# Output weights of a two-layer post-norm kernel: one block sooner, and the last two blocks as the larger of a sign and a comparison

## What is computed

```python
x = L0_attn_x                                   # 8 x 512 tokens, width 512
x = layernorm(x + x @ (W + delta_W).T)
# ternary_quant: scale = mean(|W|); clip(round(W / (scale + 1e-8)), -1, 1) * scale
z = x @ ternary_quant(W_syn).T + b_syn          # 2048 wide
thresh = top_k(z, k=204)[-1]
hidden = where(z >= thresh, relu(z), 0)
out = hidden @ ternary_quant(W_out).T + b_out
x = layernorm(layernorm(x + out, gamma, beta))
```

## Time and profile before

| | us |
|---|---|
| median of 3 runs | 633.77 (632.89 to 633.91) |
| the profiled execution | 634.05 |
| its span, from the first to the last instruction | 632.3 |
| TensorE busy | 586.0 (93%) |
| ScalarE busy | 544.0 (86%) |
| VectorE busy | 539.4 (85%) |
| GpSimd busy | 376.3 (60%) |
| granted TensorE clock, mean | 0.976 |

### The profile page before, as it was taken

How to read it: one execution, slowest core, us unless ns; L and a number is a source line. 1 busy time by engine, 2 the same in 40 slices (tenths; PEclk the granted TensorE clock), 3 DMA queues, 4 the chain that set the end, 5 groups by cost and what they waited for, 6 DMA issues and landing times.

```text
span 632.3 us, 8712 instructions
## 1 busy us (share of the span) xinstructions
PE 586.0 (93%) x2482; PEld 266.3 (42%) x2482; DVE 539.4 (85%) x657; ACT 544.0 (86%) x724; POOL 376.3 (60%) x712
## 2 busy tenths in 40 slices
PE   8799669999999999999999999999999999997573
PEld 7434324444444444444444444444444444443221
DVE  5796998998998899888888888898998888899882
ACT  1797659999999999999999999999999999989942
POOL 0126386777776547585565457545857555757773
PEclk9999789999999999999999999999999999999887
DMA  8982234545465454555454554545564454434462
GB/s 331 320 263 51 50 83 85 116 91 129 100 109 126 66 118 87 113 101 133 95 124 100 103 117 73 123 78 125 102 133 90 95 101 100 79 74 83 91 95 80
DMA packets 184581, 71.66 MB, mean 113 GB/s; under 512 B 168144, under 2 KB 176336, under 8 KB 183888
## 3 DMA queue, kind: packets, MB, share of 16 engines
q1 hardware_dynamic: 184528, 71.07, 51.2%
HBM read 20.72 MB, written 8.39 MB: 46 GB/s over the span
## 4 chain that ended last, share of the span: by engine, by line
PE 71%; DVE 8%; issue 6%; POOL 6%; ACT 3%; DMA 1%; DVEq 0%; POOLq 0%; ACTq 0%
PE z_ps L972 27%; PE o_ps L992 15%; PE u_ps L955 14%; PE o_ps L985 14%; ACT junk L542 2%; DVE w_sb L772 1%; DVE w_sb L815 1%; DVE z_sb L801 1%; POOL tmp L423 1%; DVE m L777 1%; POOL nmean L374 1%; POOL b L388 1%; ACT hh L579 1%; DVE hT L751 1%; POOL rs L384 1%
## 5 line engine op out<-in xcount | busy, mean ns | idle before, releaser
L542 ACT ACTIVATE junk<-z_sb,t_col 128x2048 f16<-128x2048 f32 x128 | 255.1, 1995 | 10.8 <-POOL t_col L442 9.8
L972 PE MATMUL z_ps<-t_syn,xhT 128*128 128x512 f16 x1024 | 231.0, 379 | 2.7 <-DVE t_syn L663 2.7
L972 PEld LDWEIGHTS z_ps<-t_syn,xhT 128*128 128x128 f16 x1024 | 99.8, 98 | 134.3 <-issue 18.1
L985 PE MATMUL o_ps<-t_out,hT 128*128 128x512 f16 x512 | 122.4, 395 | 16.8 <-DMA hT<-hh 12.4
L955 PE MATMUL u_ps<-weff,xT_sb 128*128 128x512 f32 x256 | 117.5, 602 | 2.3 <-ACT x1s L561 2.3
L992 PE MATMUL o_ps<-t_out,hT 128*128 128x512 f16 x512 | 116.1, 380 | 0.0
L423 POOL TENSOR_SCALAR tmp<-signs,dev 128x1 f32<-128x1 f32 x64 | 40.3, 629 | 124.3 <-ACT junk L542 123.4
L801 DVE SCALAR_TENSOR_TENSOR z_sb<-z_ps,sc,bias_z 128x1024 f32<-128x1024 f32 x64 | 82.0, 1280 | 18.4 <-PE z_ps L972 18.2
L772 DVE SCALAR_TENSOR_TENSOR w_sb<-z_sb,t_col 128x2048 f32<-128x2048 f32 x32 | 86.6, 2707 | 6.4 <-POOL t_col L442 6.2
L542 ACT ACTIVATE junk<-z_sb,start 128x2048 f16<-128x2048 f32 x32 | 64.0, 2001 | 29.7 <-DVE z_sb L801 29.7
L985 PEld LDWEIGHTS o_ps<-t_out,hT 128*128 128x128 f16 x512 | 51.5, 101 | 83.1 <-issue 16.0
(11 more groups left out here) (118 smaller groups left out, 605.4 us busy)
## 6 DMA issues: line engine op xcount, KB each, us to landing
xT_sb<-in_xT SPq DMA_DIRECT2D x16, 512.0 KB, 4.0
out_y<-y_sb SPq DMA_DIRECT2D x32, 256.0 KB, 2.9
z_sb<-in_w_synT SPq DMA_DIRECT2D x4, 1024.0 KB, 12.3
hh<-in_w_outT SPq DMA_DIRECT2D x2, 1024.0 KB, 9.6
z_sb<-in_w_outT SPq DMA_DIRECT2D x2, 1024.0 KB, 10.5
hT<-hh SPq DMA_TRANSPOSE x66, 4.3
weff<-in_wT SPq DMA_DIRECT2D x2, 512.0 KB, 4.7
w_sb<-in_dwT SPq DMA_DIRECT2D x2, 512.0 KB, 5.6
```

The lines of the kernel that those rows point to most:

```text
L542: a_.activation(junk[:, n % 2, :], z_sb[:, t % ZS, :], ACT.Sign, bias=at, scale=-1.0, accum_out=signs[:, j, r:r + 1]).then_inc(counted, 1)
L972: last = mm(z_ps[:, c, b * BANK:(b + 1) * BANK], xhT[:, j, h * KD + k, :], t_syn[:, k, n0:n0 + BANK], start=k == 0 and h == 0, stop=k == K ...
L985: mm(o_ps[t % OS][:, :], hT[:, j, 0, c, :], t_out[:, c, :], start=c == 0, stop=False)
```

## The change

1. On TensorE, total() for the output weights moves ahead of mm2(1,1).
2. On VectorE, out_scale and out_weights(0) move ahead of evac(1,1), and out_weights(1) from behind top8(0) to behind evac(1,1).
3. Blocks 2 and 3 are made by sign: ScalarE makes sign(w - half the scale), VectorE the comparison times -1 and then the larger of both. Block 2 takes the place between top8(0) and select(0), block 3 stands ahead of lo_h(0) and no longer behind it.
4. On ScalarE the two signs are put into stage 1: behind count(1,1) and behind ln1_out. In stages 1 and 2 count(s,3) goes ahead of hi_h(s-1).
5. On TensorE, mm3_lo of tile 0 goes ahead of flags(1).

```diff
+EARLY3 = 2
+        side_out = [hT[:, k, 1 - k, :, :].rearrange("p k t -> p (k t)") for k in range(2)]
+            def sign_out(k):
+
+                act.wait_ge(out_scaled, 1)
+                wait(act, t_out_made, k - 1)
+                a_.activation(side_out[k % 2], out_in[k], ACT.Sign, bias=sc[:, 10:11]).then_inc(over_out, 1)
+
...
                 if live(s):
                     count(s, 1)
+                    if s == 1:
+                        sign_out(2)
                     second_step(s)
...
                 if live(a):
                     ln1_out(s, a)
+                if s == 1:
+                    sign_out(3)
+                if s <= EARLY3:
+                    count(s, 3)
                 if live(s - 1):
                     hi_h(s - 1)
-                if live(s):
+                if live(s) and s > EARLY3:
                     count(s, 3)
...
+            def out_weights_by_sign(k):
+
+                wait(dve, t_out_made, k)
+                link(v.tensor_scalar(neg_out, out_in[k], sc[:, 10:11], -1.0, ALU.is_lt, ALU.mult))
+                dve.wait_ge(over_out, k - 1)
+                v.tensor_tensor(t_out[:, QB * k:QB * (k + 1), :].rearrange("p c d -> p (c d)"), side_out[k % 2], neg_out,
+                                ALU.max).then_inc(t_out_made, 1)
...
             lo_x(2)
-            evac(1, 1)
             out_scale()
             out_weights(0)
+            evac(1, 1)
+            out_weights(1)
 
             below(0)
             top8(0)
-            out_weights(1)
+            out_weights_by_sign(2)
             select(0)
...
             evac(2, 1)
-            out_weights(2)
+            out_weights_by_sign(3)
             lo_h(0)
-            out_weights(3)
...
             mm1(3)
+            total(o_ps[2][:, 0:1], part_out[:, :], part_summed, 2)
             mm2(1, 1)
-            total(o_ps[2][:, 0:1], part_out[:, :], part_summed, 2)
             mm1(4)
...
                     mm3_hi(l)
+                if l == 0:
+                    mm3_lo(l)
                 if live(f):
                     flags(f)
-                if live(l):
+                if live(l) and l > 0:
                     mm3_lo(l)
```

More of the change, by code:

```diff
@@ L175, in postln_kernel @@
         scaled = sem("scaled")
+        out_scaled = sem("out_scaled")
+        over_out = sem("over_out")
         over = sem("over")
@@ L745, in out_scale @@
                 link(v.tensor_scalar(sc[:, 9:10], sc[:, 8:9], 1e-8, 0.5, ALU.add, ALU.mult))
-                link(v.tensor_scalar(sc[:, 10:11], sc[:, 9:10], -1.0, None, ALU.mult))
+                v.tensor_scalar(sc[:, 10:11], sc[:, 9:10], -1.0, None, ALU.mult).then_inc(out_scaled, 1)
+                dve.wait_ge(out_scaled, 1)
                 link(v.tensor_scalar(sc[:, 11:12], sc[:, 5:6], sc[:, 8:9], X_SCALE / H_LIMIT, ALU.mult, ALU.mult))
```

## The result

| | before, us | changed, us |
|---|---|---|
| median, ten runs of each side by side | 633.69 (632.89 to 634.10) | 636.21 (634.80 to 640.26) |
| the profiled execution (span) | 634.05 (632.3) | 636.56 (634.8) |
| busy: TensorE, ScalarE, VectorE, GpSimd | 586.0, 544.0, 539.4, 376.3 | 585.6, 547.7, 537.8, 365.0 |

The ratio is 1.0049, with a 95% interval from 1.0037 to 1.0060: **slower by 0.5%**, 2.5 us, where 1.4 us less was forecast. The time lies above the whole range.

The account below looks back on a forecast made before the run. The prediction took the fill's chain to `ok` of tile 3, through the small engines, as the bound: 0.7 + 0.65 = 1.35 us sooner, so 633.77 - 1.35 = 632.4 us (unseen sizes: 632.4 to 633.1); range 630.8 to 634.4.

Parts of the forecast that it names:

- its L423 is held until 53.0, its last instruction until 55.5: Tile 0's second correction on GpSimd, held by VectorE's moved pair; count(0,3) then starts at about 55.7, 2.9 us late.
- The maximum: VectorE's new maximum of two fp16 tensors in blocks 2 and 3, replacing a 2.35 us instruction: 1.23 us, at most 1.39.
- tile 1's third correction: On GpSimd, three blocking VectorE instructions instead of five: about 6 us instead of 10, count(1,4) 4.4 us sooner.
- count(2,3) held hi_h(1) back: ScalarE in stage 2: hi_h(1) waits behind count(2,3) and starts at 93.9 against 94.57, so 4.4 us become 0.7.
- TensorE stopped inside mm2(4): New TensorE stop from 96.1 to 99.5, as mm2(4,1) waits for evac(3,1).
- the 0.65: First instruction of tile 3's third correction on GpSimd, 0.91 us against 0.27 free, loses up to 0.65 less.
- TensorE's lead: TensorE reaches mm2(4,0) at 92.7 instead of 99.08, 6.4 us ahead; most is lost waiting for evac(3,1).
- Its cover is the 5.47 us that ScalarE waited ahead of hi_h(0), so this lateness ends there: ScalarE's 3 us lateness up to about 67 was to be absorbed by its 5.47 us wait before hi_h(0).
- A spell at the lower clock: TensorE perhaps at 1.2 GHz after its new stop before mm2(4,1), costing up to 1.7 us; `ok` of tile 3 still decides.
- its first such pair began with L752 at 54.87: VectorE's first out_weights pair before the change; with it moved earlier, pair 1 fills idle time, 3.6 us of VectorE gained.
- the second, one more missed slot: Rival: GpSimd's tile 1 correction, or count(2,3)'s wait, loses 2.3 us; hi_h(1) at 96.2, 635.4 us; chance 0.13.
- The mechanism that the forecast rests on: While VectorE runs a two-SBUF-input instruction or SBUF-to-SBUF tensor_scalar, GpSimd is blocked; one instruction gets through between two.

Follow-up runs that it names:

- e3_pow_first: Changed kernel with one wait more: VectorE starts out_weights(0) only when GpSimd's power instruction of scales(0) is over; 633.76 us.
- e9_flag_first: Changed kernel with flags(1) ahead of mm3_lo(0) again, as in the kernel before; 635.42 us.
- e4_evac_first: Changed kernel with evac(1,1) moved back ahead of out_scale and out_weights(0), so out_weights(1) follows out_weights(0) at once; 632.90 us.
- e7_warm: Changed kernel with 24 idle matmuls of 128 columns on TensorE between mm2(2) and flags(0), their result unused; 635.36 us.
- e0_again: The changed kernel once more, unedited; 635.69 us.
- e5_pow_early1: Changed kernel with out_weights(0) waiting for GpSimd's power instruction, and EARLY3 = 1 (in stage 2 hi_h(1) ahead of count(2,3) again); 631.19 us.
- e8_move_only: Changed kernel without its signs: all four output-weight blocks by comparison alone, block 3 behind lo_h(0) again; 635.17 us.
- e11_no_signs: Changed kernel with the power-instruction wait and EARLY3 = 1, but without the two signs, block 3 behind lo_h(0); 634.36 us.

## Why the prediction was wrong, step by step

| step | predicted | after | late by |
|---|---|---|---|
| count(0,3) starts | 55.7 | 57.72 | 2.0 |
| below(0) starts | 60.3 | 62.34 | 2.0 |
| hidden(0) starts | 69.8 | 71.94 | 2.1 |
| count(1,4) starts | 81.9 | 84.05 | 2.1 |
| hidden(1) starts | 87.8 | 89.90 | 2.1 |
| hi_h(1) starts | 93.9 | 95.98 | 2.1 |
| evac(3,1) starts | 98.2 | 100.28 | 2.1 |
| flags(3) start | 122.8 | 125.07 | 2.3 |

(Counted from `var`, which came 0.31 us sooner than in before, each of these is 0.3 more.)

**One step failed first:** "its L423 is held until 53.0, its last instruction until 55.5". I let the correction begin with L423 at 50.93, where it stood in before, and left out the two instructions that GpSimd has ahead of it, the power instruction (L384 in before) and L420, now L425. L423 itself (now L428) came as said, at 52.89. But with VectorE busy from 49.02 on, the two ahead of it take the first two slots, the rest of the chain comes a short instruction later than I had it, and the last one is issued just after the gap it would have needed. It ends at 57.68, not 55.5. That is one slot, 2.0 us; e3_pow_first, which lets the power instruction through, ends it at 56.10.

**The steps behind it were right in size, and passed it on.** The maximum took 1.23 us (1.23); tile 1's third correction 6.4 us (6.0); count(2,3) held hi_h(1) back; evac(3,1) followed 4.3 us behind hi_h(1) (4.3); TensorE stopped inside mm2(4), for 2.19 us where some 3 were said, and followed `ok` of tile 3; the stages stayed at 17.47 us; GpSimd's instruction at 116.34 got back 0.49 of the 0.65. TensorE's lead was smaller than said (mm2(4,0) at 95.80, not 92.7, as mm1(5) started 2.1 us later than said and took 6.24 us), which e9_flag_first shows to count for little.

**A second statement was wrong: "Its cover is the 5.47 us that ScalarE waited ahead of hi_h(0), so this lateness ends there".** hi_h(0) started at 77.38, 5.0 us after its time before; the forecast's own 75.7 for it was 3.3 late already. ScalarE's lateness goes past hi_h(0) by way of count(1,2), tile 1's second correction (held by hidden(0)) and count(1,3), on to count(2,3): e4_evac_first, with ScalarE in time and below(0) as late as here, has hi_h(1) 4.4 us sooner counted from `var`. VectorE's lateness isn't absorbed either: from below(0) to hidden(0) it has no idle time (62.34 to 71.94 is 9.6 us; the prediction had 9.5).

**One term was mis-sized.** A spell at the lower clock was foreseen behind the stop in mm2(4), where it would have cost nothing, and put at up to 1.7 us, "what mm1(5) and mm3_hi(0) lost in rows 2"; that fits mm3_hi(0) (5.31 for 3.62), but mm1(5) lost 2.13 (5.73 for 3.60). It came behind the stop of 2.05 us ahead of flags(3), where nothing covers it: 1.64 us in the profiled execution. That stop is 1.49 us longer than the 0.56 of before, because `ok` of tile 3 came 0.90 later and TensorE was done with mm3_hi(2) 0.60 sooner. What the spell is worth in the medians stays open: e7_warm and e9_flag_first have none in their traces, and lose as much as e0_again.

**What stays open.** In e3_pow_first count(0,3) starts at 56.13 and flags(3) at 123.50, 0.4 and 0.7 us later than forecast, yet its median, 633.76, is 1.4 above 632.4. So with most of the slot given back a good part of the forecast's gain is still missing, and no run isolates what takes it. The stated range, 630.8 to 634.4, is wider than the forecast's own terms (632.4 to 633.1 with 1.0 us on both sides is 631.4 to 634.1); the measured time lies above both. One reading of the rows was loose too: "its first such pair began with L752 at 54.87" names the pair's second instruction; it began with L751:

```profile
53.55 1.29 DVE L751 TENSOR_SCALAR hT<-hh,sc 128x2048 f16<-128x2048 f32 x1
```

**The rival that came true** is the second, one more missed slot: hi_h(1) at 96.2, 635.4 us. Its size was right to 0.2 us at hi_h(1); its place was tile 0, not tile 1's correction. That its 635.4 us lies near the 635.7 and 636.2 measured is in part luck: it passed on the whole 1.6 us to the end, while in the trace 0.90 arrive at flags(3) and a spell that it didn't have adds 1.64. I gave it 0.13, because I looked for the missed slot only where the trace of before had shown them, not where the change newly put VectorE beside GpSimd. The mechanism that the forecast rests on was known; counting the slots in the new place was the work that I left undone.

A gain of that size was there to be had: e5_pow_early1 reaches 631.19 us with one wait added and one number changed.

## What to carry to other kernels

When long instructions are moved beside another engine's chain of short ones on a shared resource, write down **every** short instruction of the chain in that stretch and pair each with the gap that it gets; a margin of 0.1 us then decides about 2 us, and a small wait that lets the first one through can be worth more than it costs. Where an engine's fixed order puts an instruction with a late input ahead of one that others wait for, a speed-up further up may arrive there as nothing (the signs: nothing that can be told in one order, 3.2 us in the other). So each edit of a change is to be tried with and without the others before it is judged.

## What the runs showed of the hardware

- **A GpSimd instruction that started first was held all the same.** L389, the power instruction, started at 48.82, VectorE's L769 at 49.02; L389 took 1.52 us instead of 0.86 and ended 0.03 after it. It took 1.51 to 1.52 us in all six traces with this order, 0.86 in the eight others. The Trainium skill (SBUF — State Buffer, "Who interferes with whom") says that whoever issues first has the port for the whole instruction; here the trace differs, at least by its start times, which on GpSimd are rough. Which part of the power instruction needs the port no run here shows.
- **The other way round it holds VectorE.** In e8_move_only L766 started at 83.11, 0.03 us after GpSimd's 128x512 L398 (1.27 us), and took 3.38 us in place of 2.35 (in e11_no_signs the same, 0.03 us behind L398 and 3.38 us):

```profile
83.11 3.38 DVE L766 SCALAR_TENSOR_TENSOR t_out<-z_sb,sc,hT 128x2048 f16<-128x2048 f32 x1
```

- **The lower clock behind a stop is not certain.** In eight profiled executions TensorE's stop ahead of flags(3) was 2.05 to 2.53 us; in six of them mm3_lo behind it took 5.25 to 5.31 us, in two (e7_warm, e9_flag_first) 3.63. The stops of 0.69 to 1.69 us in four others were followed by 3.63. Inside mm2(4), 16 matmuls took 3.63 us behind stops of 2.19 us (changed) and 1.92 us (e7_warm), and 5.31 behind one of 3.09 us (e3_pow_first). That is 1.6 us by which single executions of kernels with the longer stop differ, and why their medians say more than one trace.
